# Linear attention on one core: new order of VectorE's masked attention, code conversions and output sums, and pieces of two projections between turned keys and scores

## The reference

```
q = x @ Wq + bq; k = x @ Wk + bk; v = x @ Wv + bv       # 4 heads of 128
k = k / norm(k); beta = softplus(...); alpha = sigmoid(...)
cla   = cumsum(log(alpha + 1e-06))                       # within chunks of 128 tokens
attn  = (q @ k.T) * beta * exp(cla_i - cla_j), causal
y     = attn @ v + exp(cla) * (q @ state)                # own chunk + state of earlier ones
state = state * exp(cla_end) + v.T @ (k * beta * exp(cla_end - cla))
```

## Time and profile before

| | |
|---|---|
| median of 3 runs | 962.61 us (962.59 to 963.06) |
| profiled execution, its own time | 962.71 us |
| its span | 961.0 us |
| PE busy | 942.3 us, 98% |
| DVE, ACT, POOL busy | 609.2, 459.9, 475.1 us |
| stage A, stage mid | up to 236 us, 236 to 259 us of the span |
| granted TensorE clock, mean | 0.999 |

### The profile page before, as it was taken

The page is one execution under the profiler, slowest core; times in us unless marked ns, Lnnn a source line. Parts: engine busy times, 40 slices in busy tenths (PEclk is TensorE's granted clock), DMA queues, the critical chain, the costliest instruction groups (busy, mean ns, idle before and its releaser), DMA issues.

```text
span 961.0 us, 13289 instructions
## 1 busy us (share of the span) xinstructions
PE 942.3 (98%) x4744; PEld 534.4 (56%) x4744; DVE 609.2 (63%) x1128; ACT 459.9 (48%) x918; POOL 475.1 (49%) x487
## 2 busy tenths in 40 slices
PE   6999999999999999999999999999999999999998
PEld 4888878888734454444544455444554444544443
DVE  7465565858677677776865466446466676766543
ACT  4433334356577535664443355323454665456630
POOL 5433424367457666666840043304233466665575
PEclk9999999999999999999999999999999999999999
DMA  9401300024120000000000000000000000110001
GB/s 324 161 12 34 132 22 24 1 89 132 54 78 1 1 1 1 1 1 1 1 1 1 1 1 1 1 1 1 1 1 1 1 0 1 45 44 1 1 23 67
DMA packets 14738, 30.31 MB, mean 32 GB/s; under 512 B 2064, under 2 KB 2128, under 8 KB 14672
## 3 DMA queue, kind: packets, MB, share of 16 engines
q1 hardware_dynamic: 14672, 29.45, 8.9%
HBM read 25.22 MB, written 4.23 MB: 31 GB/s over the span
## 4 chain that ended last, share of the span: by engine, by line
PE 90%; DVE 4%; ACT 2%; POOL 1%; issue 1%; DMA 0%; POOLq 0%; SPq 0%; DVEq 0%
PE psum L2057 53%; PE psum L2271 14%; PE psum L2273 13%; PE psum L2399 7%; PE psum L2088 2%; PE psum L2410 1%; DVE wv_lo L1507 1%; PE psum L2166 1%; PE psum L2077 1%; DMA xres<-x 0%; DVE xres L1609 0%; DVE state L1596 0%; ACT probs L1324 0%; DVE xb_lo L1965 0%; ACT squares L1053 0%
## 5 line engine op out<-in xcount | busy, mean ns | idle before, releaser
L869 POOL TENSOR_TENSOR hid<-hid,hid_hi 128x512 f32<-128x512 f32 x88 | 102.6, 1166 | 96.5 <-DVE hid_hi L1758 96.5
L2271 PE MATMUL psum<-xf,w_gu 128*128 128x512 f16 x352 | 133.8, 380 | 0.0
L2271 PE MATMUL psum<-xf,w_s 128*128 128x512 f16 x264 | 100.1, 379 | 1.1 <-ACT acc L1161 0.5
L2273 PE MATMUL psum<-xf,w_gu 128*128 128x512 f16 x264 | 100.1, 379 | 0.0
L1188 ACT ACTIVATE hid_lo<-hid 128x512 f16<-128x512 f32 x88 | 55.0, 625 | 40.1 <-POOL hid L869 40.1
L865 POOL TENSOR_TENSOR hid<-up,gate 128x512 f32<-128x512 f32 x44 | 56.0, 1272 | 21.9 <-ACT gate L1183 21.9
L2273 PE MATMUL psum<-xq,w_s 128*128 128x512 f16 x176 | 66.7, 379 | 0.0
L2271 PEld LDWEIGHTS psum<-xf,w_gu 128*128 128x128 f16 x352 | 34.3, 97 | 54.1 <-ACT acc L1173 15.5
L1183 ACT ACTIVATE gate<-gate,sg_xs 128x512 f32<-128x512 f32 x44 | 31.7, 721 | 58.8 <-DVE gate L1741 58.7
L731 POOL TENSOR_TENSOR xrstd<-xvar,minus_half 128x1 f32<-128x1 f32 x48 | 26.1, 547 | 65.8 <-DVE xvar L1443 65.8
L1758 DVE TENSOR_SCALAR hid_hi<-hid 128x512 f16<-128x512 f32 x88 | 39.1, 444 | 26.6 <-POOL hid L865 25.1
(11 more groups left out here) (307 smaller groups left out, 2550.5 us busy)
## 6 DMA issues: line engine op xcount, KB each, us to landing
cla_wide<-cla_dram SPq DMA_DIRECT2D x16, 256.0 KB, 3.4
out<-xres SPq DMA_DIRECT2D x16, 256.0 KB, 2.0
xres<-x SPq DMA_DIRECT2D x3, 1024.0 KB, 12.8
codes_gu<-gateT SPq DMA_DIRECT2D x1, 2816.0 KB, 11.6
codes_gu<-upT SPq DMA_DIRECT2D x1, 2816.0 KB, 9.9
codes_da<-downT SPq DMA_DIRECT2D x1, 1536.0 KB, 7.0
codes_db<-downT SPq DMA_DIRECT2D x1, 1280.0 KB, 9.9
xres<-x SPq DMA_DIRECT2D x4, 256.0 KB, 3.8
```

Source lines behind the costliest of these rows:

```text
L869: nc.gpsimd.tensor_tensor(hid[:, :], hid[:, :], hid_part(hid_hi, j, half), ALU.subtract).then_inc(rest_done, 1)
L2271: nc.tensor.matmul(bank(use[0]), w, x_operand(piece, k, False), start=start and k == 0, stop=False, skip_group_check=not start)
L2273: last = nc.tensor.matmul(bank(use[0]), w, x_operand(piece, k, True), start=False, stop=k == 1, skip_group_check=not start)
```

## The change

On VectorE: `attn_out` moves ahead of `split_lo` of the same step; the conversions move from the end of a step to behind `attn_out` and mostly one step later by the tables; `y_out` is parted in `y_state` (bank 6) ahead of `state_out`, and `y_own` (bank 7) behind it; in the last step `v_out(1, 3)` stands ahead of `attn_out`. On TensorE: of `k_rows(0, 0)` of batch 1 nine matmuls are issued in step (0,1,3), six between `k_turned` and `scores` and three behind `scores`, and three stay in place; of `v_rows(1, 3)` of batch 1 the last six are issued in step (1,1,3) between `k_turned` and `scores`. Nothing is added or removed, and SP's queue is the same.

```diff
-G_STEPS = {(0, 0, 1): (0,), (0, 0, 2): (1,), (0, 0, 3): (2,), (0, 1, 0): (3,)}
-U_STEPS = {(0, 1, 2): (2,), (0, 1, 3): (3,), (1, 0, 0): (0,), (1, 0, 1): (1,)}
+G_STEPS = {(0, 0, 2): (0,), (0, 0, 3): (1,), (0, 1, 0): (2,), (0, 1, 1): (3,)}
+U_STEPS = {(0, 1, 3): (2,), (1, 0, 0): (3,), (1, 0, 1): (0,), (1, 0, 2): (1,)}
...
-                def y_out(s, c):
+                def y_state(s, c):
...
+                def y_own(s, c):
+                    n = 4 * s + c
+                    if n > 0:
                         u.read_out((6, n - 1))
...
-                        if c < 2 and own:
-                            split_lo("A", b, l)
                         if b == 1 and (s, c) == (0, 2):
                             Use(dve, "A", 0).read_out((7, 7))
-                            dve.wait_ge(gu_ready, 8)
...
+                        if (b, s, c) == (1, 1, 3):
+                            v_out(1, 3)
                         attn_out(s, c)
+                        if c < 2 and own:
+                            split_lo("A", b, l)
+                        gate_up_weights(s, c)
+                        if b == 1 and (s, c) == (0, 2):
+                            dve.wait_ge(gu_ready, 8)
...
-                        if c < 3:
+                        if c < 3 and (b, s, c) != (1, 1, 2):
                             v_out(s, c + 1)
...
+                        y_state(s, c)
                         if (s, c) != (1, 3):
                             state_out(s, c)
+                        y_own(s, c)
                         if b == 1 and (s, c) == (1, 2):
                             query_weight_low(3)
-                        y_out(s, c)
...
-            def product(out, left, right, ks=KT):
+            def product(out, left, right, first=0, end=KT):
...
-                k_rows(0, 0)
+                k_rows(0, 0, 0 if b == 0 else 3)
...
+                        if (b, s, c) == (0, 1, 3):
+                            u.read_out(prep_use("A", 4))
+                            k_rows(0, 0, 0, 2, 1)
+                        if (b, s, c) == (1, 1, 3):
+                            v_rows(1, 3, 2)
                         scores(s, c)
-                        if c < 3:
+                        if (b, s, c) == (0, 1, 3):
+                            k_rows(0, 0, 2, 3, 1)
+                        if (b, s, c) == (1, 1, 2):
+                            v_rows(1, 3, 0, 2)
+                        elif c < 3:
                             v_rows(s, c + 1)
```

More of the change, by code:

```diff
@@ L1616, in y_out, with gate_up_weights @@
                     nc.vector.tensor_tensor(xs, xs, bank(7), ALU.add).then_inc(drained[7], 1)
+                def gate_up_weights(s, c):
+                    for k in G_STEPS.get((b, s, c), ()):
+                        dve.wait_ge(g_in, 16)
+                        nc.vector.tensor_scalar(cols(w_gu, k, HID), cols(codes_gu, k, HID), -ZERO_POINT,
+                                                None, ALU.add).then_inc(gu_ready, 1)
+                    for k in U_STEPS.get((b, s, c), ()):
+                        dve.wait_ge(u_in, 16)
+                        if k < 2:
+                            nc.vector.scalar_tensor_tensor(out=cols(w_gu, 4 + k, HID), in0=cols(codes_gu, k, HID),
+                                                           scalar=-2 * ZERO_POINT, in1=cols(codes_gu, 2 + k, HID),
+                                                           op0=ALU.add, op1=ALU.add).then_inc(gu_ready, 1)
+                        else:
+                            nc.vector.tensor_scalar(cols(w_gu, 4 + k, HID), cols(codes_gu, k, HID), -ZERO_POINT,
+                                                    None, ALU.add).then_inc(gu_ready, 1)
                 def query_weight_low(k):
@@ L1692, in _ @@
                             x_normalise(0, 0)
[L1693 to L1705, removed]
                         if c == 3 and s == 0:
@@ L2057, in mm @@
                 return nc.tensor.matmul(out, lhsT, rhs, start=start, stop=stop)
-            def product(out, left, right, ks=KT):
-                for k in range(ks):
+            def product(out, left, right, first=0, end=KT):
+                for k in range(first, end):
                     (rh, rl), (lh, ll) = right(k), left(k)
@@ L2064, in product @@
                     mm(out, lh, rl, False, False)
-                    last = mm(out, ll, rh, False, k == ks - 1)
+                    last = mm(out, ll, rh, False, k == KT - 1)
                 return last
@@ L2131, in logits_turned, with k_rows, v_rows @@
                     last.then_inc(filled[3], 1)
-                def k_rows(s, c):
+                def k_rows(s, c, first=0, end=KT, batch=b):
                     use = k_job(s, c)
[L2135 to L2140, removed]
-                    use = v_job(s, c)
[L2142 to L2145, removed]
+                    if first == 0:
+                        pe.wait_ge(wk_lo_done, KT)
+                        Use(pe, "A", batch).free(use)
+                    last = product(bank(use[0]), lambda k: xt(k, s * GROUP + c * P, P),
+                                   lambda k: pair(wqk_hi, wqk_lo, (KT + k) * D, D), first, end)
+                    if end == KT:
+                        last.then_inc(filled[use[0]], 1)
+                def v_rows(s, c, first=0, end=KT):
+                    use = v_job(s, c)
+                    if first == 0:
+                        pe.wait_ge(wv_lo_done, KT)
+                        u.free(use)
+                    last = product(bank(use[0]), lambda k: xt(k, s * GROUP + c * P, P),
+                                   lambda k: pair(wv_hi, wv_lo, k * D, D), first, end)
+                    if end == KT:
+                        last.then_inc(filled[use[0]], 1)
                 def q_cols(s, h):
```

## The result

The changed kernel takes **965.82 us** (median of 7 executions, 965.03 to 967.41), the kernel before beside it 962.61 (7 executions): a ratio of 1.0033, 95% interval 1.0023 to 1.0043. It is slower, by 3.2 us. I had forecast 963.9 in a range of 960.0 to 965.8, with "within 0.2%" the likeliest at 52%: the time lies at the range's upper edge, 965.82 against 965.8, and on the side that I gave 30%. The profiled execution took 965.82 us, with a span of 964.1.

What follows compares the result with a forecast made beforehand. TensorE, busy 98% of the span, bounds the kernel; stage A's gain is lost to the `wvT` load chain (0.0) and the clock adds 1.3, giving 964.0 on the profiled execution, forecast 963.9 us, range 960.0 to 965.8.

Steps and rivals of the forecast that it cites:

- (0,1,1), 0.78 us: Batch 0, group 1, chunk 1: TensorE's wait for `attn_out` behind `split_lo` goes, gaining 0.78 us.
- (0,1,3) and the head, net 1.6: Batch 0's last step and batch 1's head: two waits go, 1.88 us, less 0.3 for the logits' copy: net 1.6.
- (1,0,3), 0.7: Batch 1, group 0, chunk 3: TensorE's wait for `kn` at the turned keys goes, gaining 0.7 us.
- the rival to which I gave 5%: Key scaling of batch 1, group 0, chunk 3 shut out by VectorE's conversion, 0.7 us lost: 964.6 us; chance 5%.
- The sum of 3.1 us: TensorE reaches step (1,1,2) about 3.1 us earlier: 0.8 + 1.6 + 0.7, bounds 2.2 and 3.4.
- (1,1,3), another 1.1 us ahead: Batch 1, group 1, chunk 3: with six value matmuls moved there, TensorE is 1.1 us further ahead, 4.2 in all.
- The load issued 1.1 us later than before: SP's load of `wvT`, tied to the last value product's end, is issued at about 229.0, 1.1 us later.
- The chain, 0.0 net: From the `wvT` load to GpSimd's last low part: 1.1 us later issue, 1.1 shorter work, net 0.0 (-0.8 to +1.1).
- The clock, 1.3 us: TensorE's pauses in the first `wo,wvT` product lower the clock; ten slow matmuls cost 1.3 us (bounds 0 and 8.5).
- the clock stays low through the value products: Slower rival: more than eight matmuls at half speed; with 13 slow ones +3.1, so 965.7 us; chance 17%.
- the rival "faster": Chain not tied to the last value matmul, or load lands earlier and GpSimd is quicker: 958.4, half 960.5; chance 18%.
- The waits at GpSimd's pace, 4.2 us in three pieces: TensorE reaches the first `wo,wvT` product 4.2 us early and waits that long, one piece per k tile.

Runs made afterwards that it cites:

- experiment 2: Kernel before with only the last value product of batch 1 split and its copy-out moved with it: 969.38 us, ratio 1.0066.
- experiment 7: Kernel before with the four low parts of `wo` made by VectorE instead of GpSimd: 962.87 us, ratio 1.0002.
- experiment 9: Kernel before with only nine matmuls of batch 1's first key product put into step (0,1,3): 960.62 us, ratio 0.9980.
- experiment 1: Changed kernel with batch 1's last value product whole again and its copy-out back in its old place: 958.89 us, ratio 0.9960.
- experiment 3: Changed kernel with twelve useless matmuls filling both pauses, behind k tiles 1 and 2 of the first product `wo,wvT`: 962.67 us, ratio 0.9999.
- experiment 10: Changed kernel with SP's load of `s_down` held back until the first product `wo,wvT` is finished: 965.68 us, ratio 1.0033.
- experiment 4: Changed kernel with six useless matmuls behind k tile 1 only of the first product `wo,wvT`: 962.92 us, ratio 1.0001.
- experiment 5: Changed kernel with six useless matmuls behind k tile 2 only of the first product `wo,wvT`: 962.71 us, ratio 1.0005.

## Why the prediction came out as it did

- **(0,1,1), 0.78 us: right.** The wait is gone, the starts are 0.89 apart, and TensorE is 0.9 ahead one step on.
- **(0,1,3) and the head, net 1.6: 1.9 measured.** Both waits went; the 0.3 charged for the logits' copy was not due.
- **(1,0,3), 0.7: half of it, 0.3 to 0.4 measured.** The wait at the turned keys shrank from 0.57 to 0.24. VectorE's key copy did start 1.5 us earlier by TensorE's clock (165.12 where 169.72 less 3.1 is 166.6), but the chain from it to the scaled keys grew from 5.25 to 170.53 + 1.04 - 165.12 = 6.45 us. One small GpSimd instruction took 1.41 us in place of 0.23, and stood beside the conversion that the change put there:

```profile
167.63 1.41 POOL L795 TENSOR_SCALAR kscale<-sumsq 128x4 f32<-128x4 f32 x1 [2.39 <-ACT squares L1053]
```
```profile
167.35 1.62 DVE L1630 SCALAR_TENSOR_TENSOR w_gu<-codes_gu 128x1408 f16<-128x1408 int32 x1
```

  The conversion ends at 168.97, the GpSimd instruction at 169.04, with four elements per partition to work on. At (1,0,1), where the conversion starts just behind that instruction, the chain is as long: 2.79 us from it to the last scaling, 2.90 here, 1.70 before. It is the mechanism of the rival to which I gave 5%, at about half its price; the rule of the Trainium skill, "SBUF — State Buffer", section "Who interferes with whom", which I had set against the change, agrees with this pair of rows. The runs bear it out: in the ten kernels with VectorE's new order this instruction takes 1.41 us, and in the four with the old one (before and experiments 2, 7 and 9), where the conversion stands ahead of the key copy, 0.23:

```profile
172.23 0.23 POOL L795 TENSOR_SCALAR kscale<-sumsq 128x4 f32<-128x4 f32 x1 [3.91 <-ACT squares L1053]
```

  No run moved the conversion alone.
- **The sum of 3.1 us: right**, 3.2 by the turned keys. In the time, experiment 1 shows 3.9; the difference is mostly the 0.6 us of (1,1,3), which I had among the edits at nothing.
- **(1,1,3), another 1.1 us ahead: not gained.** Against experiment 1 the value pieces bring 0.0 at the first `qk` product. On the old order they bring 0.4 (experiment 2 starts it at 235.53 against 236.14, and lies 0.2 earlier from the start). That TensorE is nearly as far ahead as I had said is luck: the 0.6 of the output sums, which I had at nothing, stands in for most of the 1.1.
- **The load issued 1.1 us later than before: right**, 1.0 (228.91 against 227.89, I had said about 229.0). The new wait for `kn` is there, 0.6 idle.
- **The chain, 0.0 net: right, by two errors that cancel.** The load and what follows it until ScalarE starts took 9.5 us in place of 8.5, which I had not foreseen; so ScalarE's wait for `wo` is 7.5 us where I had said about 6. GpSimd's eight instructions shrank more than the 0.8 I took, down to the bound: all at 1.28 to 1.30 us, from 239.1 to 249.1, 10.0 us, where they took 237.1 to 249.2, 12.1 us, before. The last low part came 0.1 us earlier. Experiment 3 confirms the net, 962.67.
- **The clock, 1.3 us: this is the step that failed.** That it falls was right, and the place too (245 to 253 was said; 0.50 from 250 on). Its price by ten warm-up matmuls was taken as if only ten were slow; it measured 3.15. In the rows shown above, the eight small sums took 1.70 us, where they took 0.95 at the full clock in experiment 3, and some twelve matmuls ran 0.43 apart in place of 0.23: 0.75 + 12 x 0.2 = 3.15. This is the slower rival, "the clock stays low through the value products", 17%, worked out with 13 slow matmuls at 965.7; the kernel came out at 965.82. The two rows I had priced it by the earlier trace rows say how slow a matmul is at the lower level, and hold ten of them only since ten stood there; they don't say how long TensorE, once slow, stays so. The value nearest to the row was not the one nearest to the case. The span of 963.0 to 965.2 that I gave the forecast took in the bounds of the chain and left out those of the clock, 0 to 8.5.
- **Against the rival "faster":** it wanted the load, now alone, to land earlier. It landed later.
- **The waits at GpSimd's pace, 4.2 us in three pieces: right, 0.3 high.** TensorE reached the product at 243.18, 3.9 before the 247.1 of the kernel before, and from there to the fourth k tile at 249.13 took 5.95 us for nine matmuls of 0.23: 3.9 us of waiting. It is two pauses of 1.5 us and one of 0.2 idle, not three alike. A new wait of 0.4 for `qk_lo` stands ahead of the first `qk` product.

In the likeliest case I was right on the path and 1.9 us low on one term, and that term carried the verdict from "same" to "slower".

## What to carry to other kernels

Before work is put into a pause, look at who waits for that work's end: here a load onto the operand's memory did, and filling pauses worth 1.1 us, which brought TensorE nothing on the new order, put its issue off by 4.2. Where a gain stops at a chain without slack, ask what the engine does while it stands: here short pauses brought the clock down, and the fall cost 3.15 us on top of 3.9 of waiting; work in both of them prevented it in every execution, work in one of them in most. A price for that has to say how long the engine stays slow, and not only how slow it is.

## What the hardware did that I had not expected

- Pauses of 1.5 us brought the granted clock from 1.00 to 0.50 for 6.8 us in the changed kernel, behind the second of them; in the traces of experiments 2 and 10 it fell behind the first, and in those of experiments 4 and 5, with one such pause, it held. (The Trainium skill, "TensorE: Matmul & The Clock Gate", section "HAM oscillation — how this bites in real kernels", speaks of waits between k tiles that re-throttle the array; this trace shows such a fall with no unbroken pause above 1.7 us.)
- From SP's issue of `wvT` to ScalarE's start on it: 8.2 to 8.5 us in the six kernels with the value product whole (before among them), and 9.4 to 9.9 us in the eight with it split (the changed one among them). In the whole ones `wkT` is issued 4.1 us ahead of `wvT` and its bytes are still moving; in the split ones 8.5 us ahead, and the stretches of the changed kernel show next to no traffic for some 3 us before 228.9. That an idle queue is slower to start fits all of them, but no run kept the queue busy in a split kernel, and the other explanation I tried, the load behind it, was refuted. It stays open. Loading `wo` ahead of the wait was not tried: the kernel keeps it where the low parts of the turned x (`xt_lo`) lie, which the value product still reads.
